# Attention kernel in two-part fp32: q, k and v are split into their parts where they are made, and GpSimd takes every p_low

## The reference

```
xn = group_norm(x, 32 groups of channels)            # statistics over all tokens
q, k, v = xn @ Wq[h].T, xn @ Wk[h].T, xn @ Wv[h].T   # per head h, 64 wide
s = (q @ k.T) / 8, masked: keys up to the query (8 heads, "lb")
                     or from the query on (8 heads, "la")
o = softmax(s) @ v                                   # (2 batches, 16 heads, 2048, 64)
out = x + o.reshape(2, 2048, 1024) @ Wo.T            # heads laid side by side by reshape
```

## Time and profile before

| | |
|---|---|
| time, median of 3 runs | 3384.84 us (3383.06 to 3388.13) |
| profiled execution: time, span | 3385.93 us, 3383.9 us |
| busy: PE, PEld, DVE, ACT, POOL | 3176.5 (94%), 2494.5 (74%), 2068.3 (61%), 1740.5 (51%), 1672.6 (49%) us |
| DMA | 232.91 MB, mean 69 GB/s |
| mean granted clock of TensorE | 0.986 |

### The profile page before, as it was taken

How to read it: one execution, slowest core, us unless ns; L and a number is a source line. 1 busy time by engine, 2 the same in 40 slices (tenths; PEclk the granted TensorE clock), 3 DMA queues, 4 the chain that set the end, 5 groups by cost and what they waited for, 6 DMA issues and landing times.

```text
span 3383.9 us, 50389 instructions
## 1 busy us (share of the span) xinstructions
PE 3176.5 (94%) x14472; PEld 2494.5 (74%) x14472; DVE 2068.3 (61%) x3454; ACT 1740.5 (51%) x3525; POOL 1672.6 (49%) x1306
## 2 busy tenths in 40 slices
PE   4999998999999679999999999999999999999998
PEld 3888887788888457777777777777777777777776
DVE  6212111310110488888888888888888888888885
ACT  2100110210100267777767777777777777777774
POOL 2000000100000367777777777777777777777774
PEclk9999999999999789999999999999999999999999
DMA  6325223422311222111112111212121112111210
GB/s 236 100 84 137 93 66 82 154 71 50 97 62 48 65 83 62 59 55 44 56 50 69 44 56 50 69 44 57 51 69 44 51 56 68 45 50 57 64 37 19
DMA packets 142546, 232.91 MB, mean 69 GB/s; under 512 B 76800, under 2 KB 76800, under 8 KB 142336
## 3 DMA queue, kind: packets, MB, share of 16 engines
q1 hardware_dynamic: 142336, 230.73, 22.8%
HBM read 163.58 MB, written 67.11 MB: 68 GB/s over the span
## 4 chain that ended last, share of the span: by engine, by line
PE 28%; POOL 13%; DVE 12%; issue 9%; ACT 1%; DMA 1%; POOLq 0%; DVEq 0%; SPq 0%; ACTq 0%
POOL p_low L690 6%; POOL k L715 4%; PE acc L1059 4%; PE acc L1063 4%; PE max L1015 4%; PE acc L1061 4%; PE scores L1045 4%; PE rows L1077 3%; PE scores L1040 3%; DVE o_full L984 3%; DVE part_max L930 2%; POOL q L711 2%; DVE p_low L690 2%; DVE diagonal L701 1%; PE side L1025 1%
## 5 line engine op out<-in xcount | busy, mean ns | idle before, releaser
L690 POOL TENSOR_TENSOR p_low<-probs,p_high 128x512 fp32r<-128x512 f32 (+2 forms) x960 | 1190.9, 1258 | 573.8 <-ACT p_high L863 539.9
L859 ACT ACTIVATE probs<-scores 128x512 f32<-128x512 f32 (+3 forms) x1280 | 684.3, 535 | 410.0 <-PE scores L1045 383.6
L930 DVE TENSOR_REDUCE part_max<-max 128x1 f32<-128x512 f32 (+3 forms) x1280 | 766.1, 603 | 197.8 <-PE max L1015 175.8
L863 ACT ACTIVATE p_high<-scores 128x512 fp32r<-128x512 f32 (+3 forms) x1280 | 683.4, 534 | 0.0
L1015 PE MATMUL max<-k,q 128*128 128x512 f32 (+3 forms) x1280 | 489.5, 383 | 72.6 <-DVE part_max L930 36.0
L1059 PE MATMUL acc<-p_high,v 128*128 128x512 f32 (+3 forms) x1280 | 477.6, 373 | 28.3 <-POOL p_low L690 20.1
L318 DVE COPY stage_d<-proj 128x512 f32<-128x512 f32 x96 | 66.0, 690 | 710.9 <-PE proj L264 462.7
L1040 PE MATMUL scores<-q,k 128*128 128x512 f32 (+3 forms) x1280 | 478.0, 373 | 11.9 <-ACT p_high L863 8.9
L1045 PE MATMUL scores<-q,k 128*128 128x512 f32 (+3 forms) x1280 | 489.0, 382 | 0.0
L1063 PE MATMUL acc<-p_low,v 128*128 128x512 f32 (+3 forms) x1280 | 469.0, 366 | 0.0
L1061 PE MATMUL acc<-p_high,v 128*65 128x512 f32 (+3 forms) x1280 | 462.2, 361 | 0.0
(11 more groups left out here) (96 smaller groups left out, 5083.5 us busy)
## 6 DMA issues: line engine op xcount, KB each, us to landing
raw<-qk_s SPq DMA_DIRECT2D x256, 256.0 KB, 4.2
xs<-xT SPq DMA_DIRECT2D x64, 512.0 KB, 5.0
w_raw<-wqk SPq DMA_DIRECT2D x32, 512.0 KB, 3.7
qk_s<-stage_a SPq DMA_DIRECT2D x64, 256.0 KB, 2.4
qk_s<-stage_d SPq DMA_DIRECT2D x64, 256.0 KB, 2.4
raw<-v_s SPq DMA_DIRECT2D x64, 256.0 KB, 2.8
res<-x_res SPq DMA_DIRECT2D x32, 512.0 KB, 4.4
out<-res SPq DMA_DIRECT2D x32, 512.0 KB, 2.6
```

What stands on the lines that cost most here:

```text
L690: eng.tensor_tensor(p_low[:, n % 4, part], probs[:, n % 4, part], p_high[:, n % 4, part].bitcast(F32), ALU.subtract).then_inc(done, 1)
L859: nc.scalar.activation(probs[:, n % 4, 0:cols], scores[n % 2][:, 0:cols], ACT.Exp, scale=SCALE).then_inc(exp_done, 1)
L863: nc.scalar.activation(p_high[:, n % 4, 0:cols], scores[n % 2][:, 0:cols], ACT.Exp, scale=SCALE).then_inc(high_act, 1)
L930: nc.vector.tensor_reduce(part_max[:, s % 2, at, m:m + 1], max_bank[n % 2][:, 0:cols], AX.X, ALU.max).then_inc(max_read, 1)
```

## The change

1. In `project`, every tile now goes through both engines: ACT writes the high part to `stage_h`, then DVE writes bank minus high to `stage_l`, and SP stores both, to `qk_h` and `qk_l` (or `v_h` and `v_l`). Each stage has two slots for all tiles, where before there were two slots for each half of the tiles. PE's permission to reuse a bank comes from DVE's part.
2. In `attend`, `load_head` fetches the finished operands of a head by 8 DMAs straight into `q1, q2, k1, k2, v`. The buffer `raw`, ACT's 14 copies and the 10 subtractions are gone; PE waits for the DMAs instead.
3. `p_low` is made by GpSimd for all 40 tiles.

```diff
-        stage_a = sb("stage_a", [P, 2, NQ])
-        stage_d = sb("stage_d", [P, 2, NQ])
+        stage_h = sb("stage_h", [P, 2, NQ], F32R)
+        stage_l = sb("stage_l", [P, 2, NQ], F32R)
...
+            def store(high, low, t, n):
+                slot = t % 2
+                for dst, stage, done, stored in ((high, stage_h, out_high, stored_h), (low, stage_l, out_low, stored_l)):
+                    sp.wait_ge(done, n + 1)
+                    sp.dma_start(dst, stage[:, slot, :].bitcast(F32)).then_inc(stored[slot], 16)
...
-                            reached(pe, (out_a, out_d)[q % 2], n * 2 + (tile(b, kind, q) // 2 - 3))
+                            reached(pe, out_low, n * 4 + (tile(b, kind, q) - 7))
...
+        def high_out(eng, t, n):
+            slot = t % 2
+            eng.wait_ge(tile_done, n + 1)
+            reached(eng, stored_h[slot], n // 2 * 16)
+            reached(eng, out_low, n - 1)
+            eng.activation(stage_h[:, slot, :], bank[t % 8][:, :], ACT.Copy).then_inc(out_high, 1)
+
+        def low_out(eng, t, n):
+            slot = t % 2
+            eng.wait_ge(out_high, n + 1)
+            reached(eng, stored_l[slot], n // 2 * 16)
+            eng.tensor_tensor(stage_l[:, slot, :], bank[t % 8][:, :], stage_h[:, slot, :].bitcast(F32),
+                              ALU.subtract).then_inc(out_low, 1)
...
-                    for q in range(odd, T // NQ, 2):
-                        copy_out(eng, 4 * u + q, n * 4 + tile(b, kind, q), stage, stored, done, copy)
+                    for q in range(T // NQ):
+                        part_out(eng, 4 * u + q, n * 4 + tile(b, kind, q))
...
-HIGH_SLOT = {0: 0, 1: 1, 2: 2, 3: 3, 4: 8, 5: 9, 6: 11, 7: 14, 8: 15, 9: 16}
-K2_SLOT = {4: 8, 5: 9, 6: 10, 7: 13}
-LOW_SLOT = {n: 2 * n + 1 for n in HIGH_SLOT}
...
-LOW_DVE = (3,)
-LOW_POOL = (0, 1, 2)
+LOW_DVE = ()
+LOW_POOL = (0, 1, 2, 3)
...
+            def load_head(i, p, kind):
+                row = i + kind * PAIRS // 2
+                reached(sp, scored, count(i, p, S_TILES, -S_TILES))
+                for dst, loaded, kept, key in (
+                        (q1[0:E], first_loaded, qk_h, False), (k1[0:E], first_loaded, qk_h, True),
+                        (q1[E:P], first_loaded, qk_h, False), (k1[E:P], first_loaded, qk_l, True),
+                        (q2[0:E], second_loaded, qk_l, False), (k2[0:E], second_loaded, qk_h, True)):
+                    src = kept[bass.ds(row + key * (B * 4), 1), p * E:(p + 1) * E, :].rearrange("a e t -> (a e) t")
+                    sp.dma_start(dst[:, p, :].bitcast(F32), src).then_inc(loaded[p], 16)
+
+                reached(sp, weighed, count(i, p, S_TILES, -S_TILES))
+                for cols, kept in ((slice(0, E), v_h), (slice(2 * E, 3 * E), v_l)):
+                    sp.dma_start(v[:, p, :, cols].bitcast(F32),
+                                 kept[bass.ds(2 * i + p, 1)].rearrange("a p t e -> (a p) t e")).then_inc(v_loaded[p], 16)
...
-                        pe.wait_ge(low_split, count(i, p, SPLITS, 8))
+                        pe.wait_ge(first_loaded[p], 64 * (i + 1))
...
+                    if n == 0:
+
+                        pe.wait_ge(second_loaded[p], 32 * (i + 1))
...
-                        pe.wait_ge(low_split, count(i, p, SPLITS, SPLITS))
+                        pe.wait_ge(v_loaded[p], 32 * (i + 1))
```

More of the change, by code:

```diff
@@ L336, in weights_and_tiles @@
                 blocks(eng, b == B - 1 and kind == KINDS - 1, one)
-                for t in range(odd, TOK, 2):
+                for t in range(TOK):
                     if not high and b == 0 and kind == 0:
-                        count_x(1, t - 1)
                         count_x(1, t)
-                    copy_out(eng, t, tile(b, kind, V_TILES + t), stage, stored, done, copy)
+                    part_out(eng, t, tile(b, kind, V_TILES + t))
         def count_x(b, h):
@@ L511, in slots @@
                 plan.append(("round " + part, False, half))
-        for step, at_slot in (("k2 high", K2_SLOT), ("split high", HIGH_SLOT), ("split low", LOW_SLOT)):
-            for n, at in at_slot.items():
-                if at == t and has_next:
-                    plan.append((step, True, n))
         for n, at in OP_SLOT.items():
@@ L529, in prologue @@
 def prologue():
-    return ([(step, False, n) for n in range(SPLITS) for step in ("k2 high", "split high", "split low")
-             if step != "k2 high" or n in K2_SLOT]
-            + [("max", False, n) for n in range(4)] + [("diagonal", False, 0), ("shift", False, 0)]
+    return ([("max", False, n) for n in range(4)] + [("diagonal", False, 0), ("shift", False, 0)]
             + [("max", False, n) for n in range(4, 12)] + [("diagonal", False, 1),
@@ L809, in do @@
             def do(step, kind, i, p, n):
-                if step == "split low" and not first_head(i, p):
-                    u, h = n // 2, n % 2
-                    slot = (p * RAW_UNITS + u) % 2
-                    pool.wait_ge(act_split, count(i, p, SPLITS, n + 1))
-                    reached(pool, low_split, count(i, p, SPLITS, n))
-                    wait_one(pool, low_pool, LOW_POOL, i, p, LOW_SLOT[n] + AHEAD - S_TILES)
-                    split_low(pool, p, slot, u, h)
-                    pool.wait_ge(low_split, count(i, p, SPLITS, n + 1))
-                elif step == "scores" and n % 4 in LOW_POOL:
+                if step == "scores" and n % 4 in LOW_POOL:
                     low_part(pool, low_pool, kind, i, p, n)
@@ L944, in do @@
                         both_parts(kind, i, p, S_TILES - 1)
-                elif step == "split low" and first_head(i, p):
-                    dve.wait_ge(act_split, n + 1)
-                    reached(dve, low_split, n)
-                    split_low(dve, p, n // 2 % 2, n // 2, n % 2)
                 elif step == "weights":
@@ L1082, in _, with build @@
             heads(pe, do)
-def build(nc, xT, x_res, wqk, wv, wo, qk_s, v_s, out):
-    project(nc, xT, wqk, wv, qk_s, v_s)
-    attend(nc, x_res, wo, qk_s, v_s, out)
+def build(nc, xT, x_res, wqk, wv, wo, qk_h, qk_l, v_h, v_l, out):
+    project(nc, xT, wqk, wv, qk_h, qk_l, v_h, v_l)
+    attend(nc, x_res, wo, qk_h, qk_l, v_h, v_l, out)
 def kernel(**inputs):
```

111 lines of the change are left out of this document (25 added, 86 removed).

## The result

The changed kernel takes 3405.18 us (median of 4 runs, 3400.93 to 3409.36) beside 3384.24 for the kernel before: ratio 1.0053, 95% interval 1.0041 to 1.0066. The forecast was 3270, faster. The profiled execution has 3403.49 us, 17.6 more than that of before. First the page of the kernel after: span, busy time by engine, clock by fortieths, and a few of its costliest groups (busy, mean ns | idle before, releaser).

The account below looks back on a forecast made before the run. PE was taken as nearly the bound, with about 5 us of waits a head. Heads 99 + 2.6, head 0 15, start of `attend` 5, less 6.5 in `project`, made 115 us won: 3270 us, case range 3234 to 3315.

Parts of the forecast that it names:

- They are issued when the scores of the head before are done, in its slot 37: Slot 17 of `attend`: operand loads issued some 35 us ahead arrive in time, so the wait for k's split goes, 0.5 us.
- The rival that named this queue of 4 MB: Turn of heads: a 4 MB queue delays the load of x or q past slot 17; 3370 to 3400 us, chance 0.05.
- In the steady state 5.44 us a tile cover that: `project`: PE's tile time covers a tile's wait for the store two back; loss only at first blocks and batch ends, 6.5 us.
- The first blocks: `project`, after `both_first_blocks`: the third weight block comes late behind stores; PE loses 2.6 us in both batches, 5.2 together.
- Slot 30, "0.5": Slot 30 of a head: DVE's p_low of tile 31 no longer waits behind the division; 0.5 us won a head.
- Slots 0 to 8, "1.9": Slots 0 to 8: DVE sheds two p_low and collides less with POOL (0.5); 1.9 us won a head, bounds 1.4 to 2.6.
- Slots 14 and 17: Slot 14: x's addition no longer behind DVE's p_low, 0.2 us; slot 17: wait for k's split gone, 0.5 us a head.
- I charge nothing: Slots 24 to 35: POOL making every p_low keeps up with PE's 1.39 us a tile, gaining at least 0.12; no cost.
- The rival "POOL becomes the bound": Full tiles of `attend`: collisions with DVE make POOL's p_low late; 3417 us, or 3340 at half the excess; chance 0.09.
- Head 0 and the start of `attend`: Head 0 loses its split and load waits, 15 us won (8 to 20); first maximum at 1135.2, 5 us won (2 to 8).
- The 256-byte pieces of v: v's transfers, in twice as many small pieces: 0.2 us each, 60 us ahead of use; nothing in the sum.
- The likeliest case: Whole kernel: small waits removed and other terms sum to 115 us won; 3270 us, 3234 to 3315, chance 0.55.

Follow-up runs that it names:

- the run without it: Changed kernel with the next batch's x loads running four tiles ahead in the first batch's v tiles: 3382.61 us, 0.9995 of the kernel before.
- the run without them: Changed kernel with the third weight block split ahead of the way out of the first four tiles: 3393.06 us, 1.0021 of the kernel before.
- the two runs that gave POOL its pause back: Changed kernel with p_low back on DVE, for every fourth tile: 3386.85 us; for tile 31 only: 3388.92 us.

## Why the prediction was wrong, step by step

- **"They are issued when the scores of the head before are done, in its slot 37"** is the step that failed most. The time of issue was right; what I read from it was only that the data would be in time for slot 17, which it was. I had the loop's turn before me ("66 to 67 at a loop's turn") and did not ask what a burst of 3 MB does to the turn's own transfers. Price: 59 us of the 133. The rival that named this queue of 4 MB had it delay x or q; it got 0.05, and its place was wrong; that the time lies only 5 us above its 3370 to 3400 is luck.
- **"In the steady state 5.44 us a tile cover that"** held for q and k tiles and failed for the 16 v tiles of batch 0, where another load sits in the same queue. The step lacked a count of what else SP and DVE do between two tiles. Price: 22.6 us in the run without it, 20 of them the step and 2.7 slower products behind it. The rest of the 30 is the next point and 1.5 us ahead of the first product, which starts at 36.2 to 38.4 us in these runs, whatever the kernel.
- **The first blocks**, 2.6 us twice: the mechanism was right, the size was not. PE lost 3.9 us twice, and the rest of the 12.1 that the run without them won lies in slower products behind the two, at half the clock.
- **Slot 30, "0.5"**: wrong sign. The slot went from 1.93 to 2.56 us, and the two runs that gave POOL its pause back brought it to 1.92. The wait on p_low of tile 31 went, and its place was taken by one on the reductions behind a longer division. Here I had charged the collisions to POOL alone and nothing to DVE. Price: 1.1 us a head, 34 of the 43.
- **Slots 0 to 8, "1.9"**: 1.3 in the mean of the plain heads: slots 4 and 8 are 0.8 shorter each, slot 5 is 1.0 longer. DVE's two p_low there did go, but the collision term of 0.5 did not come; `o_full` took 2.88 us against 2.89, and the `diagonal` 1.24 against 1.26. My lower bound was 1.4.
- **Slots 14 and 17**: 0.2 and 0.8 came back, for 0.2 and 0.5; the wait for the split of k is gone, and no wait for an operand's DMA took its place there.
- **"I charge nothing"** for POOL's pace: right. PE waited 0.4 us for p_low in the whole program. But it was close: in the run of 12 ten tiles took 13.78 us without a gap, 1.38 each against PE's 1.39, where I had expected 1.25 to 1.3 and a gain of 0.12 a tile. The rival "POOL becomes the bound" named the right sign with the wrong mechanism.
- **Head 0 and the start of `attend`**: -17.5 for -15, and -5.9 for -5. Both matches owe something to luck. Head 0 is 3 to 5 us slower in most other executions. Of the 5.9 only 3.5 are in PE's step to the first maximum, which fell from 21.1 to 17.6 where I had 16 (it waits for the DMA of k's low part, 17.25 us; by the terms given, 1123.41 + 0.7 + 1.4 + 9.3, my 1135.2 should also have been 1134.8); the other 2.4 come between there and the first value product, where I had counted nothing.
- **The 256-byte pieces of v** cost nothing that a row shows, as said.
- The likeliest case was a sum of small things: of 115 us, 99 were counted as small waits removed, and each was taken at its full size. Of the 133 us that it missed, 59 at the turns and 20 in the hole lie where the sum had no term at all, so no bound of its terms could hold them.

## What to carry to other kernels

When transfers become larger and fewer, ask at each issue what else must pass the same engines in the next 8 us; the instructions of a loop's next pass are such a transfer, and an "issue" wait of several us on two engines at once is how the profile showed it here. Moving the issue by eight tiles, one line, was worth 67 us. When a store is made to wait for a later engine, follow the queue that holds it round to whatever that engine waits for: the ring here took 7.06 us a tile, 4.7 of them one landing, while DVE and SP were mostly idle. And an engine that gets all of a job loses its gaps; where two engines slow each other, one tile of forty in the right slot was worth nine tenths of what ten brought.

## What the runs showed of the hardware

- At the turn of head 10, instructions of the loop's next pass arrived 5 us later than with no burst behind operand loads of 512 KB each, after 1.73 MB of 3 MB had moved, and 4.7 us later after 1.57 MB of 1.57; DVE and ACT stood still for 8.3 and 8.3 us, and for 7.0 and 7.1. With no burst DVE stood for 2.3 us, and the turn costs 1.6 us over a plain head.
- At each of the ten turns of the kernel after PE stood for 6.4 to 7.5 us, and its clock went to the 1.2 GHz level within that wait, for 6.8 to 10.2 us.
- Head 0 took 68.4 us in the run with the loads eight tiles late and 73.4 with them four tiles late, though the two kernels are alike there. In the second the granted clock fell to half for 6.8 us twice within the head, where PE had been waiting for DVE's reductions. The same code so differs by 5 us from one execution to the next.
- Where a `diagonal` of DVE (two inputs in SBUF) and a p_low of POOL overlap, the one that starts second is longer: with DVE 0.03 to 0.04 us ahead they take 0.68 and 1.79 us, with POOL 0.13 to 0.14 us ahead 1.70 and 1.29 (medians of 30 heads each). A half of `o_full` takes 0.62 us in the median where POOL runs during less than half of it, and 1.6 where it runs during more, in the kernel after.
